# FFN weights turned by transposing transfers of the sync queue instead of by TensorE

## What is computed

```python
q, k, v = x @ wq.T + bq, x @ wk.T + bk, x @ wv.T + bv
q2, k2, v2 = q @ wiq.T + biq, k @ wik.T + bik, v @ wiv.T + biv   # 16 heads of 64
attn = softmax(q2 k2^T / 8 + mask)       # mask: softplus(type weight) on edges, -inf elsewhere
x = x + (attn v2) @ wo.T + bo            # on _layernorm(x)

def _weight_fake_quant(w):
    scale = max|w| over each row / 127
    return clip(round(w / scale), -128, 127) * scale
h = act_fake_quant(silu(xq @ w_gate_q.T) * (xq @ w_up_q.T))
x = x + h @ w_down_q.T                   # w_gate, w_up: (352, 1024); w_down: (1024, 352)
```

## Time and profile before

| | us |
|---|---|
| median of 3 runs | 334.89 |
| lowest, highest | 334.47, 343.88 |
| the profiled execution, whole | 333.7 |
| its span (first to last instruction) | 331.9 |
| PE busy in the span | 321.3 |
| mean granted clock of PE | 0.997 of full |

### The profile page before, as it was taken

One profiled execution on the slowest core, in us unless ns is written; L12 is line 12 of the kernel. 1 busy time (PEld: TensorE's weight loads), 2 busy tenths in 40 slices (PEclk: granted clock), 3 DMA queues, 4 the chain that ended last, 5 costly groups with the idle time before them and its releaser, 6 DMA issues.

```text
span 331.9 us, 5960 instructions
## 1 busy us (share of the span) xinstructions
PE 321.3 (97%) x2071; PEld 296.4 (89%) x2072; DVE 223.9 (67%) x597; ACT 181.8 (55%) x332; POOL 190.7 (57%) x256
## 2 busy tenths in 40 slices
PE   5999999999999999999999999999999999999993
PEld 5899998878999999999999999999999878888852
DVE  3857899776255555553185978879797876497573
ACT  4857357474333333333375968678595866244562
POOL 6686678457777776789816483563727757100004
PEclk9999999999999999999999999999999999999998
DMA  7997334757233443583421241403113110000005
GB/s 257 371 404 284 126 129 138 244 181 250 61 126 130 126 126 127 162 289 130 140 65 64 64 139 52 128 8 121 63 64 128 59 71 0 0 2 0 2 0 192
DMA packets 16395, 41.72 MB, mean 126 GB/s; under 512 B 3456, under 2 KB 6640, under 8 KB 16368
## 3 DMA queue, kind: packets, MB, share of 16 engines
q1 hardware_dynamic: 12656, 38.08, 33.3%
q0 software_dynamic: 2064, 1.80, 2.0%
q10 hardware_dynamic: 1648, 1.48, 1.3%
HBM read 37.99 MB, written 3.37 MB: 125 GB/s over the span
## 4 chain that ended last, share of the span: by engine, by line
PE 91%; DVE 3%; POOL 2%; ACT 1%; issue 1%; POOLq 0%; DVEq 0%
PE PS L773 68%; PE PS L930 5%; PE PS L918 5%; PE PS L906 4%; PE PS L754 2%; PE PS L1069 1%; PE PS L764 1%; PE PS L842 1%; PE PS L832 1%; PE PS L817 1%; PE PS L836 1%; PE PS L807 1%; POOL X L495 1%; POOL QT L466 1%; DVE V L1532 1%
## 5 line engine op out<-in xcount | busy, mean ns | idle before, releaser
L428 POOL TENSOR_TENSOR ring<-stage,ring 128x256 fp32r<-128x256 f32 x124 | 91.3, 771 | 39.8 <-ACT ring L516 37.0
L773 PE MATMUL PS<-XT,ring 128*128 128x384 f32 x528 | 93.3, 335 | 0.0
L773 PEld LDWEIGHTS PS<-XT,ring 128*128 128x128 f32 x528 | 91.4, 188 | 0.1
L446 POOL DMA_INDIRECT codes<-ecol,place x51 | 59.2, 1160 | 25.5 <-issue 15.4
L516 ACT ACTIVATE ring<-stage 128x1024 fp32r<-128x1024 f32 x52 | 54.3, 1057 | 6.0 <-PE PS L773 3.8
L623 ACT ACTIVATE scratch<-scratch,smx 128x384 f32<-128x384 f32 x48 | 29.0, 607 | 18.5 <-DVE smx L1367 18.5
L773 PE MATMUL PS<-QT,ring 128*128 128x384 f32 x192 | 35.5, 338 | 0.0
L773 PE MATMUL PS<-AT,ring 128*128 128x384 f32 x192 | 35.2, 338 | 0.0
L773 PEld LDWEIGHTS PS<-AT,ring 128*128 128x128 f32 x192 | 33.0, 188 | 1.5 <-issue 1.5
L773 PE MATMUL PS<-ring,AT 128*128 128x512 f32 x144 | 34.0, 393 | 0.0
L1271 DVE TENSOR_TENSOR ring<-stage,ring 128x1024 fp32r<-128x1024 f32 x21 | 25.7, 1227 | 12.1 <-issue 7.8
(11 more groups left out here) (202 smaller groups left out, 479.9 us busy)
## 6 DMA issues: line engine op xcount, KB each, us to landing
stage<-in_weights SPq DMA_DIRECT2D x56, 512.0 KB
V<-in_w_gate_up SPq DMA_DIRECT2D x4, 512.0 KB, 7.2
codes<-scratch SPq DMA_DIRECT2D x3, 576.0 KB, 14.9
X<-in_x SPq DMA_DIRECT2D x3, 512.0 KB, 5.0
scratch<-codes POOLq DMA_DIRECT2D x2, 576.0 KB, 6.0
scratch<-in_w_gate_up SPq DMA_DIRECT2D x2, 512.0 KB
V<-in_w_down SPq DMA_DIRECT2D x5, 176.0 KB, 5.2
codes<-ecol,place POOLq DMA_INDIRECT x51
```

Source lines behind the costliest of these rows:

```text
L428: ins = pool.tensor_tensor(ring[1][:, slot, piece], stage[:, slot % STAGE, piece], ring[0][:, slot, piece].bitcast(F32), ALU.subtract)
L446: pool.indirect_dma_start(codes[b].rearrange("(n a) -> n a", a=1), bass.IndirectOffsetOnAxis(ap=place[:, t:t + 1], axis=0), ecol[:, VAL, t ...
L773: ins = pe.matmul(outs, lhs[a], rhs[b], start=start and n == 0, stop=stop and n == 2, skip_group_check=True)
```

## The change

The six groups of `ffn_turn` transposes on PE and the 24 transposes of `w_down` in the tail go, with ACT's `down_take`. ACT now writes the bf16 rows back into the landing buffer itself, `gu_rows` and `dn_rows` (`ffn_take`), and SP issues `dma_start_transpose` transfers from the buffer into `guT` and `wdT` (`turn_rows`): 14 in all, eight of 128 x 384 for `w_down`, four of 128 x 1024 and two of 96 x 1024 for gate and up. A landing buffer is free for the next load when its transfers have landed (`BUF_FREE`), and SP waits for that in `load_ffn`. ACT packs steps 0 and 1 during chunks 4 and 6, and step s + 2 during chunk 8 + s. In the tail PE runs `keep_clock(8, ...)` where the 24 transposes stood. `edges_over(0)` and `(1)` come after chunks 30 and 31, and `edges_over(2)` after `q_low(0)`.

```diff
-        wdN = sb("wdN", [P, KT, I_F], BF16)
+        wdT = sb("wdT", [P, IT, C], BF16)
+        gu_rows = [a[:, 0, :].bitcast(BF16) for a in gu_in]
+        dn_rows = [a.bitcast(BF16)[:, 0:IT * P] for a in dn_in]
+        ROWS_PACKED = (2, 4, 6, 7, 9, 11, 13, 14)
+        BUF_FREE = {3: 0, 4: 1, 5: 2, 6: 4, 7: 5}
-            def load_ffn(s, taken):
-                if taken:
-                    sp.wait_ge(ffn_evac, taken)
+            def load_ffn(s):
+                if s in BUF_FREE:
+                    sp.wait_ge(rows_turned[BUF_FREE[s]], 32)
+            def turn_rows(s):
+                i, j, buf = s // 4, s % 4, FFN_BUF[s]
+                sp.wait_ge(rows_packed, ROWS_PACKED[s])
+                sp.dma_start_transpose(wdT[:, :, s * P:(s + 1) * P], dn_rows[buf]).then_inc(rows_turned[s], 16)
+                if j < IT:
+                    i0, iw = I_TILES[j]
+                    sp.dma_start_transpose(guT[:, :, I_F * i + i0:I_F * i + i0 + iw], gu_rows[buf][0:iw, :]
+                                           ).then_inc(rows_turned[s], 16)
-            for c in range(10, 13):
-                next_chunk(c)
-            load_ffn(3, 1)
+            turn_rows(0)
+            next_chunk(10)
+            next_chunk(11)
+            turn_rows(1)
+            load_ffn(3)
+            next_chunk(12)
+            turn_rows(2)
+            load_ffn(4)
             next_chunk(13)
-            load_ffn(4, 2)
-            load_ffn(5, 3)
+            load_ffn(5)
             next_chunk(14)
+            turn_rows(3)
             next_chunk(15)
-            load_ffn(6, 4)
+            turn_rows(4)
+            load_ffn(6)
             next_chunk(16)
-            load_ffn(7, 5)
-            for c in range(17, 20):
-                next_chunk(c)
+            turn_rows(5)
+            load_ffn(7)
+            next_chunk(17)
+            turn_rows(6)
+            next_chunk(18)
+            turn_rows(7)
+            next_chunk(19)
...
-            pool.wait_ge(ffn_full, 6)
-            pool.wait_ge(down_packed, 8)
+            pool.wait_ge(rows_turned[5], 32)
+            pool.wait_ge(rows_turned[7], 16)
...
-                act.activation(wdN[:, s, :], dn_half[FFN_BUF[s]], ACT.Identity, bias=minus[:, 0:1]).then_inc(down_packed, 1)
+                act.activation(dn_rows[buf][:, 0:I_F], dn_half[buf], ACT.Identity, bias=minus[:, 0:1]
+                               ).then_inc(rows_packed, 1)
                 if j < IT:
-                    act.wait_ge(ffn_full, IT * i + j + 1)
-                    act.activation(guT[:, :, I_F * i + i0:I_F * i + i0 + iw], gu_ps[:, :, 0:iw], ACT.Identity,
-                                   bias=minus[:, 0:1]).then_inc(ffn_evac, 1)
+                    act.activation(gu_rows[buf][0:iw, :].rearrange("p (b c) -> p b c", b=2), gu_half[buf][0:iw, :, :],
+                                   ACT.Identity, bias=minus[0:iw, 0:1]).then_inc(rows_packed, 1)
...
-            for i, (i0, iw) in enumerate(I_TILES):
-                ...
-                    ins = pe.transpose(dn_ps(i)[0:iw, s * P:(s + 1) * P], wdN[:, s, i0:i0 + iw], wide[:, 2 * P:3 * P])
+            keep_clock(8, red_columns, 6)
...
+            for s in range(5, 7):
+                k_tile(s)
             edges_over(0)
-            k_tile(5)
+            k_tile(7)
             edges_over(1)
-            k_tile(6)
-            edges_over(2)
-            k_tile(7)
...
             q_low(0)
+            edges_over(2)
             k_low(0)
```

More of the change, by code:

```diff
@@ L232, in gnn_ffn @@
         ffn_q = sem("ffn_q")
[L233 to L237, removed]
+        rows_turned = [sem(f"rows_turned{s}") for s in range(KT)]
+        rows_packed = sem("rows_packed")
         up_seen = sem("up_seen")
@@ L339, in _ @@
             sp.wait_ge(t_full, KT)
-            load_ffn(0, 0)
-            load_ffn(1, 0)
+            load_ffn(0)
+            load_ffn(1)
             next_chunk(4)
-            load_ffn(2, 0)
+            load_ffn(2)
             next_chunk(5)
@@ L565, in ffn_take @@
             def ffn_take(s):
-                i, j = s // 4, s % 4
+                i, j, buf = s // 4, s % 4, FFN_BUF[s]
                 act.wait_ge(ffn_q, s + 1)
-                act.activation(wdN[:, s, :], dn_half[FFN_BUF[s]], ACT.Identity, bias=minus[:, 0:1]).then_inc(down_packed, 1)
+                act.activation(dn_rows[buf][:, 0:I_F], dn_half[buf], ACT.Identity, bias=minus[:, 0:1]
+                               ).then_inc(rows_packed, 1)
                 if j < IT:
-                    i0, iw = I_TILES[j]
-                    act.wait_ge(ffn_full, IT * i + j + 1)
-                    act.activation(guT[:, :, I_F * i + i0:I_F * i + i0 + iw], gu_ps[:, :, 0:iw], ACT.Identity,
-                                   bias=minus[:, 0:1]).then_inc(ffn_evac, 1)
+                    iw = I_TILES[j][1]
+                    act.activation(gu_rows[buf][0:iw, :].rearrange("p (b c) -> p b c", b=2), gu_half[buf][0:iw, :, :],
+                                   ACT.Identity, bias=minus[0:iw, 0:1]).then_inc(rows_packed, 1)
             for s in range(8):
@@ L584, in _ @@
                     act.activation(clip[:, 1, :], clip[:, 0, :], ACT.Exp, scale=-1.0).then_inc(soft_in, 1)
-                elif s == 7:
-                    ffn_take(0)
+                elif s in (4, 6):
+                    ffn_take(s // 2 - 2)
                 act.wait_ge(w_used, RING + s + 1)
@@ L592, in _ @@
                 high((s + CIV + AHEAD) // STAGE, s + CIV + AHEAD, (s + AHEAD) % RING)
-                if s < 7:
-                    ffn_take(s + 1)
+                if s < 6:
+                    ffn_take(s + 2)
                 if s % 4 == 3:
-                    act.wait_ge(ffn_full, (4, 6)[s // 4])
-                    act.wait_ge(down_packed, (5, 8)[s // 4])
+                    act.wait_ge(rows_turned[(3, 6)[s // 4]], (16, 32)[s // 4])
                     for m in range(NT):
@@ L719, in _ @@
                                scale=wsc[0:iw, 0, i:i + 1]).then_inc(sig_ready, 1)
[L721 to L728, removed]
             act.wait_ge(h_scale, 1)
@@ L732, in _ @@
                                scale=gmx[0:iw, 12:13]).then_inc(ht_ready, 1)
-            down_take(2)
             act.wait_ge(dsc_ready, 1)
@@ L795, in project @@
                 finish(part(slot, slot % 2, src, range(KT)))
[L797 to L809, removed]
             def keys(g):
@@ L865, in _ @@
                         keys(g)
-                if s > 5:
-                    ffn_turn(s - 6)
             for c in range(8):
@@ L886, in _ @@
                 finish(ins)
-                if c < 6:
-                    ffn_turn(c + 2)
             pe.wait_ge(acc_free, NT + 1)
@@ L1075, in _ @@
             low_half, high_half = range(4), range(4, KT)
+            for s in range(KT):
+                pe.wait_ge(rows_turned[s], 32 if s % 4 < IT else 16)
             for part in range(2):
@@ L1104, in _ @@
                         gate_up(g, i, high_half).then_inc(gu_full, 1)
-            for i, (i0, iw) in enumerate(I_TILES):
[L1106 to L1110, removed]
-                    ins = pe.transpose(dn_ps(i)[0:iw, s * P:(s + 1) * P], wdN[:, s, i0:i0 + iw], wide[:, 2 * P:3 * P])
-                ins.then_inc(down_full, 1)
+            keep_clock(8, red_columns, 6)
             spread_max(1, 8, NT + 1)
@@ L1117, in down_in @@
             def down_in(i):
-                pe.wait_ge(down_ready, max(i + 1, 2))
                 pe.wait_ge(hq_ready, i + 1)
```

## The result

| | before | changed |
|---|---|---|
| time, median of 5 runs each on one chip, us | 335.98 (334.47 to 343.88) | 339.96 (338.64 to 347.98) |
| ratio to before, 95% interval | | 1.0135 (1.0094 to 1.0175) |
| profiled execution, us | 333.7 | 338.64 |
| its span, us | 331.9 | 336.9 |

The changed kernel is 1.35% slower: clear of the noise, but under the 2% from which a difference is counted. 340.3 us and 1.6% were forecast. The ratio leaves out one execution of each kernel (343.88 and 347.98 us) that ran in a slower state. The median of the kernel before differs between groups of runs (334.01 to 335.98 us), so all that follows compares ratios taken within a group, or rows of single profiles.

What follows compares the result with a forecast made beforehand. PE was taken as the bound (321.3 of 331.9 us busy). Wait +5.9, clock +2.2, transposes -2.55 and tail -0.1 gave +5.45: 339.2 us profiled, 340.3 median, range 332.5 to 350.

Steps and rivals of the forecast that it cites:

- D: Delay that two transposing transfers put on what follows in SP's queue, such as load_ffn(4) behind turn_rows(2): 3.7 us.
- L: Time from issue of a transposing pair to its last landing, which load_ffn(6) waits out behind turn_rows(4): 5.5 us.
- PE stands: PE's wait ahead of chunk 14 for low(14), forecast as D + L - 3.3: 5.9 us.
- clock: PE's granted clock falls during the wait ahead of chunk 14; running at half pace afterwards costs 2.2 us.
- transposes saved: Six groups of FFN transposes leave PE in the woven-in weights stretch: 2.55 us gained.
- in the tail: The 24 w_down transposes there are worth nothing, but dropping ACT's third down_take gains 0.1 us.
- the priced terms together: Sum of wait at chunk 14, clock cost, transposes saved and tail gain: +5.45 us.
- rival 1: Transposing transfers cost what plain ones do: PE stands 0.9 us, clock stays up, net -1.75, 333.1 us; chance 0.23.
- The second loop: The same round trip through steps 5 and 7, ahead of chunk 15: costs L - 6.0 us if L exceeds 6.0; forecast nothing.
- Rival 3: Transposing transfers slower still, over 5 us of delay per pair, both loops costing: 350, 372 or more; chance 0.23.
- Rival 4: POOL's scatter held up by the transfers, delaying PE at chunk 31: up to 7 us more, 347; chance 0.10.
- The edge tables: Moved overlays of 1.75 us of DVE each, around chunks 30, 31 and q_low(0), fall into DVE's idle gaps: price 0.

Runs made afterwards that it cites:

- c1: Changed kernel with step 4 in a fourth buffer and loaded early, step 6 in step 1's buffer, step 7 in step 4's: 331.35 us, 0.9915 of before.
- a1: Changed kernel with load_ffn(4) and chunk 13 issued ahead of turn_rows(2): 1.002 of before.
- a3: Changed kernel with 27 matmuls of zeros on PE between chunks 13 and 14: 1.0094 of before.
- b0: The changed kernel measured again, nothing altered (its second profile): 1.0116 of before, span 336.5 us.
- a4: Changed kernel with turn_rows(4) issued twice and load_ffn(6) waiting for both: 1.0224 of before.
- b3: The kernel before with only the edge-table overlays moved as in the change: 0.9989 of before.
- a2: Changed kernel with step 6 landing in a fourth buffer, its load issued ahead of turn_rows(3): 0.9987 of before.
- c2: c1 with the three edge-table overlays back in their old place: 0.9993 of before.

## Why the prediction was right

It hit the place and the mechanism, and the size in part by luck: one gap ahead of chunk 14, released by DVE's `low`, DVE waiting on step 6's `w_down`, SP standing between `turn_rows(4)` and `load_ffn(6)`, half pace behind. Step by step:

| step | predicted | measured |
|---|---|---|
| `turn_rows(2)` starts | 54.7 | 55.44 |
| D | 3.7 | 2.56 |
| issue of `load_ffn(4)` to DVE's start | 5.1 | 4.6 |
| `turn_rows(4)` issued (64.6 + D) | 68.3 | 67.45 |
| L | 5.5 | 4.42 |
| landing of step 6 | 4.1 | 4.31 |
| PE stands | 5.9 | 4.40 |
| clock | 2.2 | 2.0 |
| transposes saved | 2.55 | 2.55 by the rows of before; c1 begins chunk 16 2.76 earlier |
| in the tail | 0.1 | 0.08 |
| the priced terms together | +5.45 | +3.77 |
| whole profiled execution | +5.45 | +4.94 |

The priced terms came to 1.7 us less than forecast. The whole came nearer only because 1.2 us more stand in places that the forecast left out: 0.2 by chunk 16, 0.37 at 133 us, 0.37 behind PE's last matmuls and the rest spread. That part of the agreement is luck. So is the nearness of the medians (340.3 and 339.96), since the kernel before measured 335.98 beside it and not the 334.9 that the forecast added to: the ratio says 4.5 us, the forecast 5.4.

**The terms mis-sized are D and L**, 1.1 us each, and both were worked out from one price. I put the price in the pieces of the transfer: 256 bytes at 42 ns, 3.7 us for a pair. The size of the pieces was right, the price wasn't. DMA totals and queue 1 of before's page, then of the changed kernel's:

```profile
DMA packets 16395, 41.72 MB, mean 126 GB/s; under 512 B 3456, under 2 KB 6640, under 8 KB 16368
...
q1 hardware_dynamic: 12656, 38.08, 33.3%
```

```profile
DMA packets 25547, 43.94 MB, mean 130 GB/s; under 512 B 12608, under 2 KB 15792, under 8 KB 25520
...
q1 hardware_dynamic: 21808, 40.31, 36.5%
```

9152 packets and 2.23 MB more, 244 bytes each, and all of them under 512 B. Their time is 0.365 x 16 x 336.9 - 0.333 x 16 x 331.9 = 199 us of one engine, 22 ns each, or some 1.9 us for a pair on 16 engines. That is shorter than the two issues. It is an estimate, since it puts every change of queue 1 down to these packets: the same sum gives 25 ns in the second profile (37.1%) and 30 in a1 and a3 (38.2 and 38.0%), which is 2.6 us for a pair, about what the two issues take. What stood ahead of `load_ffn(4)` was the issuing: 1.19 us for 128 x 384 and 1.29 for 128 x 1024, whatever the size, against 0.33 to 0.59 for a plain load. L is likewise the first issue (1.2) and the second transfer's landing, whose median over the run is 3.1 us. The packet of queue q10 was the nearest row in size, but a wrong one: it belongs to other work, and 1.48 MB in 1648 packets are 898 bytes each, not 256. Both errors go one way and made 2.2 us, and the step from `load_ffn(4)` to DVE another 0.5; against them stand 0.7 for the later start of `turn_rows(2)` and small ones, so that the gap came out 1.5 short.

The Trainium skill, page "VectorE: DVE Perf Modes", section "The three transpose paths", has 1309 ns for one 128 x 128 block, which simply added up was 14.4 us for a pair of 11 blocks. That sum doesn't agree with the trace: a pair lands in 4.42 us, both issues included. What a lone block takes no run here shows. The Trainium skill, page "Advanced Engine Details and Errata", section "X-Bar Transpose (TRN2)", says that transposing DMAs are as fast as regular ones. The trace doesn't bear that out for these: 244 bytes in 22 ns on each of 16 engines are, by the estimate above, 177 GB/s, half of the 356 in the earlier trace rows (less at 25 or 30 ns), and the issue is two to four times a plain one.

**The clock**, taken over from the start of the kernel, came to 2.0 (2.7 in the second profile) against 2.2. One premise was off: the earlier trace rows had it fall 3.6 us after the work ended, and rival 1 leaned on that, but in the gap ahead of chunk 14 it fell after 2.0 (2.7 in the second profile, 3.0 in a1).

**The second loop** was held to be free up to L = 6, with the same L as the first. The bound holds up, the one L doesn't: behind `turn_rows(5)` it was 5.72, and the loop was free; 6.68 in the second profile and 7.99 in a3 aren't under 6, and by the same working would cost 0.7 and 2.0 us where chunk 14 runs at full pace (1.0 by b0's rows, 1.47 measured in a3). So clock and loop aren't independent terms: what a full clock gives back, a slow second loop can take.

**Rival 1** (plain transfers) needed D + L under 5.9, and it came to 6.98. **Rival 3** didn't occur, but a4 went halfway there, with L at 9.1. **Rival 4** didn't decide in the changed kernel, where PE is late itself. Its last scatter starts at 135.68 in one profile and at 139.28 in the other (before: 136.96), so a lateness of some us, not of 16.8, seems to be real. It decides in c1, once PE is some 7 us earlier there than in the changed kernel (chunk 16 at 84.08 against 90.88). **The edge tables** were priced at nothing, which b3 confirms for PE's old pace. What this left out is the other side: the move is worth 0.8% in c1, where PE runs ahead and the tables land later.

## What to carry to other kernels

A pair of transposing transfers held its queue here for 2.5 us, as long as the DMA engines worked on it (1.9 to 2.6) or longer: count 1.2 to 1.3 us of issue for each, put plain loads that someone waits for ahead of them, and don't let a load that will be wanted soon wait for one that was just issued; against the changed kernel, another buffer was worth 1.5% here (a2), and 2.2% with the order (c1). When a change takes work off the bounding engine and lengthens a round trip, work out the second and third loop behind the first as well, since with the first one cut they left gaps of 1.73 and 1.26 us here. And judge two parts of a change together: a step that measures as nothing alone (the tables) may be what lets the other one pay.

## What the runs showed of the hardware that I had not expected

- The issue of a transposing transfer on SP's queue took 1.18 to 1.32 us in most places, the longer ones for 128 x 1024. Elsewhere it took up to 2.94 us (c1 at 75.73; 1.29 at the same place in c2). What makes it longer isn't shown.
- Transfers issued behind 1.7 MB of plain loads landed 7.16 us after the first issue instead of 4.42 (a1); the same pair behind 1.2 MB took 5.72, 6.68 and 7.99 in three profiles (the changed kernel, b0, a3).
- What an idle time of PE cost in clock, by the length of the gap: nothing behind 1.47, 1.73 and 1.76 us (a3, a2, c1); 1.5 behind 2.98 (c2); 1.3 us behind 3.51 (a1: 9.66 for two chunks of 4.18); 2.7 behind 3.69 (b0); 2.0 behind 4.40 (the changed kernel); 2.2 behind 11.27 (a4). Once the level had fallen the price was 1.3 to 2.7 us, and it didn't follow the length of the gap.
- ACT stood for 3.5 to 5.6 us between projection chunks in some profiles with no releaser on record, in kernels with and without the change. Its cause is open.
